# Edge scatter by matrix products: destination blocks of 8 nodes instead of 16, and one of its three operands made by GpSimd

## The reference, cut to what matters

```python
a = leaky_relu(sum((h[src] + e) * attn), 0.01)     # one score per edge
a = exp(a - segment_max(a, dst)[dst])
a = a / (segment_sum(a, dst)[dst] + 1e-16)
out = relu(segment_sum(h[src] * a[..., None], dst))
dst = min(3125 * uniform ** 2, ...), sorted        # many edges at low node numbers
```

## Time and profile before

| stretch of the profiled execution, us | what it is | PE busy | DVE busy | ACT busy | POOL busy | PE clock granted |
|---|---|---|---|---|---|---|
| 0 to 52.3 | prepare | 13.48 | 35.59 | 5.57 | 3.40 | 1.00 |
| 52.3 to 336 | node projection, edge attributes | 193.13 | 220.19 | 241.95 | 254.99 | 0.57 |
| 336 to 378.5 | end of the edge softmax | 13.79 | 23.50 | 7.56 | 18.50 | 0.50 |
| 386.2 to 928.6 | the matrices | 511.59 | 440.76 | 330.56 | 0.00 | 0.99 |
| 928.6 to 4057.4 | the rest, unchanged | | | | | |

### The profile page before, as it was taken

One profiled execution on the slowest core, in us unless ns is written; L12 is line 12 of the kernel. 1 busy time (PEld: TensorE's weight loads), 2 busy tenths in 40 slices (PEclk: granted clock), 3 DMA queues, 4 the chain that ended last, 5 costly groups with the idle time before them and its releaser, 6 DMA issues. The chain is left out here.

```text
span 4057.4 us, 72126 instructions
## 1 busy us (share of the span) xinstructions
PE 3512.4 (87%) x21551; PEld 2863.7 (71%) x21552; DVE 2649.1 (65%) x5840; ACT 2534.4 (62%) x6497; POOL 817.1 (20%) x459
## 2 busy tenths in 40 slices
PE   5764999998995999998599999999999977999365
PEld 3332555556884899997488888888888866888244
DVE  6876888781114200003899999999999537997324
ACT  3992256792111344444699999999999677996132
POOL 2994000000001411110211111111111101110342
PEclk9555999999997999997799999999999988998588
DMA  4981033455334211213211111111110162330324
GB/s 116 220 208 40 32 129 162 194 226 212 145 114 145 59 38 61 78 57 109 104 49 48 48 48 48 48 48 48 48 48 33 47 218 74 121 129 27 100 73 149
DMA packets 111916, 395.79 MB, mean 98 GB/s; under 512 B 16364, under 2 KB 70422, under 8 KB 88518
## 3 DMA queue, kind: packets, MB, share of 16 engines
q1 hardware_dynamic: 97728, 356.56, 25.4%
q0 software_dynamic: 11696, 31.60, 2.6%
q10 hardware_dynamic: 2368, 6.03, 0.6%
HBM read 268.97 MB, written 125.18 MB: 97 GB/s over the span
## 5 line engine op out<-in xcount | busy, mean ns | idle before, releaser
L1406 PE MATMUL gat_agg<-f_XN,gat_A 128*128 128x257 f32 x5000 | 1109.4, 380 | 20.2 <-DVE gat_A L1523 20.2
L1406 PEld LDWEIGHTS gat_agg<-f_XN,gat_A 128*128 128x128 f32 x5000 | 938.5, 190 | 154.9 <-DVE gat_A L1523 20.8
L1327 ACT ACTIVATE kept_X<-kept_X,gat_s 128x128 f32<-128x128 f32 x2500 | 741.3, 390 | 73.1 <-DVE kept_X L1512 73.1
L880 PE MATMUL mat_cw<-mat_join,mat_lane 128*128 128x400 f16 x2976 | 511.6, 334 | 33.2 <-issue 18.6
L1272 POOL TENSOR_TENSOR kept_X<-gat_low,gat_r 128x1024 f32<-128x1024 f32 x100 | 242.8, 2428 | 1144.7 <-DVE gat_A L1523 692.2
L880 PEld LDWEIGHTS mat_cw<-mat_join,mat_lane 128*128 128x128 f16 x2976 | 291.4, 98 | 253.9 <-issue 47.8
L2491 ACT ACTIVATE moe_exp_h<-moe_exp_hbank,w_b1c 128x128 f32<-128x128 f32 x632 | 231.6, 368 | 366.0 <-PE moe_exp_hbank L2435 299.8
L1512 DVE SCALAR_TENSOR_TENSOR kept_X<-gat_r,gat_s 128x128 f32<-128x128 f32 x1700 | 459.0, 348 | 1.1
L2444 PE MATMUL moe_exp_ybank<-moe_exp_w2b,moe_exp_h 128*128 128x256 f32 x1484 | 353.4, 387 | 52.1 <-issue 50.6
L1523 DVE SCALAR_TENSOR_TENSOR gat_A<-kept_X,early_C 128x1664 f32<-128x1664 f32 x200 | 354.5, 1814 | 0.1
L1476 DVE CUSTOM_DVE_ANT_0 gat_junk<-gat_als,gat_absT 128x3200 bf16<-128x3200 f32 x100 | 348.1, 3481 | 9.8 <-PE gat_absT L1382 5.9
(11 more groups left out here) (388 smaller groups left out, 4823.6 us busy)
## 6 DMA issues: line engine op xcount, KB each, us to landing
count_matrix<-w_wide SPq DMA_DIRECT2D x25, 1600.0 KB, 5.2
weight_matrix<-w_wide SPq DMA_DIRECT2D x25, 1600.0 KB, 8.8
early_C<-count_matrix SPq DMA_DIRECT2D x25, 1600.0 KB, 6.7
late_C<-count_matrix SPq DMA_DIRECT2D x25, 1600.0 KB, 6.7
w_wide<-in_edge_attr_dram SPq DMA_DIRECT2D x50, 768.0 KB, 6.1
e_WT<-weight_matrix SPq DMA_DIRECT2D x13, 1600.0 KB, 6.8
sum_more<-weight_matrix SPq DMA_DIRECT2D x12, 1600.0 KB, 6.5
moe_exp_xgT<-slot_rows SPq DMA_DIRECT2D x20, 640.0 KB, 9.5
```

Of the source, the lines that this page charges most:

```text
L880: last = nc.tensor.matmul(cw[:, bass.ds(bank + min(w, 1) * 512, JW)], lane[:, b, w, n, :], join[:, b, n, :], start=False, stop=False, skip ...
L1327: last = nc.scalar.activation(w, w, ACT.Exp, bias=s02[:, t, h:h + 1])
L1406: last = nc.tensor.matmul(agg[h % 2][:, 0:D + 1], A[h % 2][:, t, :], g.XN[:, t, :], start=(t == 0), stop=(t == NT - 1))
```

## The change

1. **Blocks of 8 nodes.** `DB` = 8, so `NB` = 400, `JW` = 200, `SLOTS` = 1184 (74 sets of 16), `GROUPS` = 10 groups of 128 items for the gathers.
2. **One bank for a block.** The weights' 200 columns and the counts' 200 columns stand side by side in one bank, `BANKS` = 8 in turn. ACT drains two banks at once (`PAIRS` = 8 in a tile): 200 times 128 x 800, as before, from another layout.
3. **High weights on the other operand.** `join` is two pieces side by side: the one-hot, and the one-hot times the high weight. One product of 400 columns with the plain lane one-hot gives high weights and counts. A second product of 200 columns, low lanes with the plain `join` one-hot, adds the low weights.
4. **One operation for 16 `join` one-hots** on DVE (a two-input comparison 128x16x200 with the keys doubled to f16 pairs) in place of 16 scalar operations, and a second for the multiplication by the high weight.
5. **POOL makes the low lanes**: one multiplication 128x2048 f16 a set, behind `lane_ready`. PE waits for it by a semaphore of its own, `low_ready`.
6. In `prepare` the table of block starts is made another way (one reduction over 4000 columns instead of two over 1600), and some buffers lie elsewhere.

```diff
-DB = 16
+DB = 8
 NB = NT * P // DB
-SUB = P // DB
+PAIRS = P // (2 * DB)
...
-            link(nc.vector.tensor_tensor(mask, mask, all_groups(sd_wide[:, 1, :]), ALU.mult))
-            link(nc.vector.tensor_reduce(c_n[:, :], mask, AX_X, ALU.add))
+            link(nc.vector.scalar_tensor_tensor(out=c_n[:, :], in0=b_n[:, :], scalar=-1.0, in1=slotn[:, :],
+                                                op0=ALU.mult, op1=ALU.add))
...
-        join = k.sb("join", [P, 2, U, JW], F16)
-        lane = k.sb("lane", [P, 2, 3, U, P], F16)
+        join = k.sb("join", [P, 2, U, 2, JW], F16)
+        lane = k.sb("lane", [P, 2, 2, U, P], F16)
...
                     dve.wait_ge(item_done, it * U + (b + 1) * U)
                     items = bass.ds(it * U + b * U, U)
-                    nc.vector.tensor_tensor(pairs(lane[:, b, 0, :, :]),
-                                            g.iota_lo[:, :].rearrange("p (o l t) -> p o l t", o=1, t=2)
-                                            .to_broadcast([P, U, P // 2, 2]),
-                                            every_pair(g.item_lo[:, items, :]), ALU.is_equal).then_inc(lane_ready, 1)
-                    for n in range(U):
-                        nc.vector.tensor_scalar(join[:, b, n, :], g.iota_join[:, :], g.item_key[:, at(it * U + (b * U + n))],
-                                                None, ALU.is_equal)
-                    dve.wait_ge(lane_ready, it + (b + 1))
-                    for n in range(2):
-                        last = nc.vector.tensor_tensor(pairs(lane[:, b, n + 1, :, :]), pairs(lane[:, b, 0, :, :]),
-                                                       every_pair(g.PT[:, n, items, :]), ALU.mult)
-                    last.then_inc(set_ready, 1)
+                    nc.vector.tensor_tensor(pairs(lane[:, b, 0, :, :]), iota_pairs(g.iota_lo[:, :], P),
+                                            every_pair(g.item_lo[:, items, :], P), ALU.is_equal).then_inc(lane_ready, 1)
+                    nc.vector.tensor_tensor(pairs(join[:, b, :, 1, :]), iota_pairs(g.iota_join[:, :], JW),
+                                            every_pair(g.item_key[:, items, :], JW), ALU.is_equal).then_inc(join_ready, 1)
+                    dve.wait_ge(join_ready, it + (b + 1))
+                    nc.vector.tensor_tensor(pairs(join[:, b, :, 0, :]), pairs(join[:, b, :, 1, :]),
+                                            every_pair(g.PT[:, 0, items, :], JW), ALU.mult).then_inc(set_ready, 1)
+
+        @block.gpsimd
+        def _(pool):
+            with strides(pool, SLOTS // U, 2) as it:
+                for b in range(2):
+
+                    wait_alone(pool, lane_ready, it + (b + 1))
+                    items = bass.ds(it * U + b * U, U)
+                    nc.gpsimd.tensor_tensor(lane[:, b, 1, :, :], lane[:, b, 0, :, :],
+                                            g.PT[:, 1, items, 0:1].to_broadcast([P, U, P]), ALU.mult).then_inc(low_ready, 1)
...
                         if n == 0:
                             pe.wait_ge(set_ready, it + (b + 1))
+                            pe.wait_ge(low_ready, it + (b + 1))
 
                         pe.wait_ge(drained, mine)
-                        for w in range(3):
-                            last = nc.tensor.matmul(cw[:, bass.ds(bank + min(w, 1) * 512, JW)], lane[:, b, w, n, :],
-                                                    join[:, b, n, :], start=False, stop=False, skip_group_check=True)
-                        last.then_inc(item_done, 1)
+                        nc.tensor.matmul(cw[:, bass.ds(bank, 2 * JW)], lane[:, b, 0, n, :],
+                                         join[:, b, n, :, :].rearrange("p w j -> p (w j)"), start=False, stop=False,
+                                         skip_group_check=True)
+                        nc.tensor.matmul(cw[:, bass.ds(bank, JW)], lane[:, b, 1, n, :], join[:, b, n, 1, :],
+                                         start=False, stop=False, skip_group_check=True).then_inc(item_done, 1)
...
-            act.sem_inc(drained, SETS)
+
+            act.sem_inc(drained, BANKS + 1)
...
-                nc.scalar.activation(both[:, odd, :, :].rearrange("p w (h d) -> p w h d", d=P)[:, :, :, s * DB:(s + 1) * DB],
-                                     cw[:, bank:bank + 1024].rearrange("p (w j) -> p w j", w=2)[:, :, 0:JW]
-                                     .rearrange("p w (h j) -> p w h j", j=DB), ACT.Copy).then_inc(copied, 1)
+                first = (s + 1) % (BANKS // 2) * 1024
+                pair = cw[:, first:first + 1024].rearrange("p (e n) -> p e n", e=2)[:, :, 0:2 * JW]
+                nc.scalar.activation(both[:, odd, :, :].rearrange("p w (h d) -> p (w h) d", d=P)
+                                     [:, :, s * 2 * DB:(s + 1) * 2 * DB].rearrange("p r (e j) -> p e r j", e=2),
+                                     pair.rearrange("p e (r j) -> p e r j", j=DB), ACT.Copy).then_inc(copied, 1)
...
-                g.item_key = e.sb("item_key", [P, GROUPS * P])
+                g.item_key = e.sb("item_key", [P, GROUPS * P, 2], F16)
```

More of the change, by code:

```diff
@@ L131, in prepare @@
         ends = k.sb("ends", [1, 2])
-        bound_i = k.sb("bound_i", [ER, NB], I32)
-        bound = k.sb("bound", [ER, NB])
+        bound_i = whole_buffer(g.raw[5], ER)[:, EW:EW + NB].bitcast(I32)
+        bound = whole_buffer(g.raw[5], ER)[:, EW + NB:EW + 2 * NB]
         below = k.sb("below", [ER, NB])
@@ L139, in prepare @@
         c_n = k.sb("c_n", [P, GROUPS])
-        sd_wide = k.sb("sd_wide", [P, 2, NB])
-        sd = k.sb("sd", [1, 2, NB])
-        u = k.sb("u", [1, NB])
-        turned = [k.ps(f"turned{c}", [P, 512]) for c in range(KD)]
+        starts_wide = k.sb("starts_wide", [P, NB])
+        starts = k.sb("starts", [1, NB])
+        turned_bank = k.ps("turned", [P, 512])
+        turned = [turned_bank[:, c * D:(c + 1) * D] for c in range(KD)]
         turned_hi = [k.ps(f"turned_hi{b}", [P, 512]) for b in range(2)]
@@ L224, in _ @@
             act.wait_ge(wide_ready, 1)
-            nc.scalar.activation(sd_wide[:, :, :].rearrange("p w b -> p (w b)"), wide[:, 0:2 * NB], ACT.Copy).then_inc(wide_kept, 1)
+            nc.scalar.activation(starts_wide[:, :], wide[:, 0:NB], ACT.Copy).then_inc(wide_kept, 1)
             act.wait_ge(rooms_free, 1)
@@ L242, in _ @@
             pe.wait_ge(ones_ready, 1)
-            pe.wait_ge(sd_ready, 1)
-            nc.tensor.matmul(wide[:, 0:2 * NB], g.ones[0:1, :], sd[:, :, :].rearrange("o w b -> o (w b)"),
-                             start=True, stop=True).then_inc(wide_ready, 1)
+            pe.wait_ge(starts_ready, 1)
+            nc.tensor.matmul(wide[:, 0:NB], g.ones[0:1, :], starts[:, :], start=True, stop=True).then_inc(wide_ready, 1)
             pe.wait_ge(loaded, 96)
@@ L341, in _ @@
             dve.wait_ge(row_ready, 1)
-            nc.vector.tensor_copy(g.item_block[:, :], row[:, 0:GROUPS * P])
+            nc.vector.tensor_scalar(g.item_block[:, :], row[:, 0:GROUPS * P], 1.0, None, ALU.add)
             dve.wait_ge(hi_kept, EC)
@@ L583, in edge_softmax, with after_raw @@
         last_piece = g.WT[0:ER, 1, EW + CH:2 * EW + CH]
-        def after_raw(b, rows, n, first=0):
-            return whole_buffer(g.raw[b], rows)[:, first:first + n]
+        def after_raw(first, rows, n):
+            return g.wide[0:rows, first:first + n]
         def per_group(t):
@@ L592, in all_edges @@
             return col.rearrange("p (g o) -> p g o", o=1).to_broadcast([P, GROUPS, P])
[L593 to L599 removed]
+        score_r, run, top, prob = (after_raw(n * EW, ER, EW) for n in range(4))
+        lines = after_raw(4 * EW, 1, 4 * ER)
+        carry = after_raw(4 * EW + 4 * ER, 1, 2 * ER + 2).rearrange("p (w r) -> p w r", w=2)
+        tables = 4 * EW + 6 * ER + P
+        lo_s, key_s, packed, prob_s = (per_group(after_raw(tables + n * GROUPS * P, P, GROUPS * P)) for n in range(4))
+        part_i = per_group(after_raw(tables + 4 * GROUPS * P, P, GROUPS * P).bitcast(I32))
+        packed_i = per_group(after_raw(tables + GROUPS * P, P, GROUPS * P).bitcast(I32))
+        prob_it = after_raw(tables + 5 * GROUPS * P, P, GROUPS * P)
         fetched, split_ready = k.sem("fetched"), k.sem("split_ready")
@@ L655, in _ @@
                 act.wait_ge(turned_ready, m + 1)
-                nc.scalar.activation(g.item_key[:, n * P:(n + 1) * P], turned[m % 2][:, 0:P], ACT.Copy).then_inc(copied, 1)
+                nc.scalar.activation(g.item_key[:, n * P:(n + 1) * P, :], twice(turned[m % 2][:, 0:P]),
+                                     ACT.Copy).then_inc(copied, 1)
             for n in range(GROUPS):
@@ L801 @@
 WEIGHT_SCALE = 16384.0
-SETS = 4
+BANKS = 8
 ROWS_IN = 4
@@ L825, in edge_matrices, with pairs, every_pair, iota_pairs @@
         AHEAD = 2 * U
-        def pairs(lanes):
-            return lanes.rearrange("p u (l t) -> p u l t", t=2)
-        def every_pair(values):
-            return values.rearrange("p (u o) t -> p u o t", o=1).to_broadcast([P, U, P // 2, 2])
+        def pairs(hot):
```

(7 more changed lines are left out.)

72 lines of the change are left out of this document (32 added, 40 removed).

## The result

The changed kernel takes 4255.03 us (median of four runs), the kernel before in the same comparison 4058.36 us: ratio 1.0488, interval [1.0473, 1.0503]. A second comparison, on another occasion, gave 1.0473 [1.0454, 1.0491]. It is slower by 4.9%. The forecast was 4202, with 4160 to 4345 as the likeliest case's own range.

What follows compares the result with a forecast made beforehand. DVE and POOL taking turns were to bound the matrices stage: 74 sets at 9.2 us plus the end make 686.5 us, +136.7; with +6.6 around it, 4057.4 becomes 4200.7, and 4202 with 1.1 for the median. Range 4035 to 4345.

Steps and rivals of the forecast that it cites:

- likeliest case: Matrices stage: DVE and POOL take turns, 9.2 us a set; 4202 us, own range 4160 to 4345, chance 0.72.
- What bounds: Matrices stage: DVE's operations and POOL's multiplication, one after the other, set the pace of each set at 9.2 us.
- exclusion: DVE operations with two SBUF inputs and POOL's multiplication hold each other off completely, on f16 as on f32.
- DVE's L852: Sign in the matrices stage: this DVE line near 6 us, with POOL's operation inside it.
- first rival: Matrices stage: f16 operations don't exclude each other, 5.05 to 5.6 us a set; about 3940 us, chance 0.15.
- DVE's terms: DVE in a set: lane one-hot 1.14 us, two operations of 1.78, some 0.1 between; together 4.8 us.
- POOL's term: POOL's low-lane multiplication in a set: 4.53 us as for f32 additions, exclusive part 4.38 us.
- second rival: POOL's multiplication twice as fast on f16, still exclusive: 7.0 us a set, 4039 us, chance 0.06.
- PE hidden: PE's 4.1 to 5.2 us a set lie beside the making of the next set and don't set the pace.
- The sum: Matrices stage: 74 sets at 9.2 us plus the end, 686.5 us against 549.8, +136.7 us.
- Around it: Outside the matrices stage: `prepare` +2.5 us and the softmax's end +4.1 us, together +6.6 us.
- fourth rival: PE granted 1.2 GHz: 8.2 us a set, hidden under 9.2; without exclusion it bounds, 4133 us, chance 0.02.

Runs made afterwards that it cites:

- in-turn: The changed kernel with 32-bit block numbers, plus semaphores making POOL's multiplication wait for the join one-hot and DVE's multiplication wait for POOL's: 4174.7 us, ratio 1.0283.
- write-only: The changed kernel with 32-bit block numbers, but POOL fills the low lanes with zeros (memset) instead of multiplying: 4003.9 us, ratio 0.9862.
- the run with the longer stores: The changed kernel (16-bit block numbers) with the weights' row of each tile stored a second time to a spare array: 4306.7 us, ratio 1.0608.

## Why the prediction was right, and where not

**What bounds.** The direction and the time were right, the bound was not. The forecast had DVE and POOL, taking turns, set the pace of every set. They do take turns: exclusion holds on f16, the first operation holds the other off completely, and one 3.2 us wait a set stands in DVE's L852 (I had looked for it near 6 us). The first rival, 3940, is refuted by the in-turn and the write-only runs together. But in the changed kernel this is hidden behind PE's sequencer, and taking it away leaves the stage at 732.2 us. It becomes the pace only once the load is short.

**DVE's terms.** Right: 1.14 for the lane one-hot; two operations over 3200 columns, forecast 1.78 and measured 1.82 and 1.83; a wait of 0.1 us between.

**POOL's term.** Mis-sized. I took the f32 addition's 4.53 us, exclusive 4.38; on this multiplication it is 3.61, exclusive 3.46. That is 0.92 us of the 1.16 by which a set of DVE and POOL, at 8.02, is shorter than the forecast's 9.18. The rest is overlap that the sum left out: the wait of 0.12 us between DVE's two operations lies inside POOL's 3.46, and DVE's multiplication ends 1.69 us after POOL's, with the next lane one-hot starting 0.08 ahead of its end. Together 1.16 x 74 = 86 us less. The second rival guessed 2.3 us for POOL. What gives the 20% is not told apart: the type, the operation and the broadcast second input all differ from the earlier trace rows. The Trainium skill ("GPSIMD Engine Reference", section 2.1 "Instruction dispatch") says that a two-input body takes at most one operand a cycle. The cost per element and not per byte that I took from it fits the 3.61 us better than a halving does, and not exactly.

**PE hidden.** This is the step that failed: "4.1 to 5.2 us of set s lie beside the making of set s+1". The products do. I counted FUSED_REGOPS of 74 ns among the register work and overlooked the load of the 16 numbers, which stood in the same sequencer for 1.1 us a set, and the change of its table's type, which I took for one of the edits that only move or shrink buffers. With the 16-bit load PE's sequencer needs 3.8 us and 4.3 to 4.8 behind it, 8.30 in all where no store runs, and up to 13.9 beside one; over the stage 9.6 a set on average (709.6 / 74). That is more than DVE and POOL's 8.02, and it lifts the stage from the 604.5 us with 32-bit numbers to 730.4.

**The sum.** Forecast +136.7; -87.3 for the pace (74 x 8.02 against 74 x 9.2), +5.3 at the stage's ends (604.5 - 74 x 8.02 = 11.0 against 5.7), and +125.9 from there to the pace of the loads, makes the measured +180.6. That the time fell inside the likeliest case's own range was luck: two misses of opposite sign hid each other. The forecast mechanism by itself, the run with 32-bit numbers, gives +62 us, a ratio of 1.016. The long loads by themselves, with low lanes on DVE, give +190 us, all of the slowdown.

**Around it.** Prepare +2.2 (forecast 2.5, first addition of edge attributes 54.53 against 52.31), the softmax's end +5.4 (forecast 4.1): the two more gathers cost 3.2 us, the turns and casts behind the last gather 2.2 (13.15 us to the first set against 10.97). The other 7.6 did not come back in any later profile and are no effect of the change.

**The clock.** The fourth rival was half there: 0.79 granted over the stage, with 0.50 us an item after each pause, then 0.255. Under the 8.02 us of DVE and POOL it costs nothing, as forecast (0.86 in the run with 32-bit numbers, every period at 8.02 but the first, 7.95). Nor does it show in the pace of the changed kernel. In the set above the slow products end at 620.03, 2.4 us late, but the sequencer had handed them on and begun its next load at 617.47, 4.36 us after the last one's end, as in the sets at full speed.

## What to carry to other kernels

Read what an engine's sequencer does (register loads among it) as part of the engine's time: idle that "issue" ends can be work, and it is then found under the line's own instructions, not in a wait list. Ask of each byte saved in a table who reads it and in what width. And where a change has two costs, undo them one at a time and then together: here, in the stage, the one alone gave 126 us back, the other nothing, both 229, which turned the loss into a gain (0.991).

## What the runs showed of the hardware that was not expected

- A register load of 16 values by PE's sequencer takes 1.107 us from a 32-bit and 3.788 us from a 16-bit table; of 8 32-bit values 0.59 us. That is 0.07 us a value against 0.24.
- Stores to memory in flight stretch it, up to 3.2 times: 3.6 us (32-bit, 16 values), 1.8 (8 values), 12.1 (16-bit, in the run with the longer stores, at a DMA busy share of 0.97). The Trainium skill ("SBUF — State Buffer", section "Who interferes with whom") says that DMA never contends with a compute engine. For DVE's and POOL's operations that agrees (L852 from 5022 to 5029 ns and L862 from 4927 to 4965 over all 74, with and without stores beside them); for the sequencer's register load these runs show otherwise. By what path it reads is not shown.
- PE plays on from its queue through a 1.1 us load when products are 0.51 us an item (period 8.12 us with the load at 1.1 and at 0.59), but not through one of 3.8 us (periods of 9.4 us and more in the kernel before with 16-bit numbers).
- POOL filled 128x2048 f16 in 1.80 us each of 74 times beside DVE's two-input operation, and DVE's was no longer for it.
